# The first attention of a four-stage transformer kernel: another order of its instructions on four engines, and other PSUM banks

## What is computed

```python
h = _layernorm(x, axis=-1) * (1 + ca) + sa
x = x + ga * _L0_attn_ref(h, ...)
# inside: x = rmsnorm(h); 16 query heads, 8 key/value heads of 64
q = (x @ Wq).reshape(b, n, QH, DH).transpose(0, 2, 1, 3)
kv = x @ Wkv
q = _mh_rmsnorm(q, q_gamma)          # every head normalised to length 1, times a gamma
k = _mh_rmsnorm(k, k_gamma)
sim = jnp.tanh(sim / SOFTCLAMP) * SOFTCLAMP * DH ** (-0.5)
sim = jnp.where(causal, neg, sim); attn = jax.nn.softmax(sim, axis=-1)
out = jnp.einsum('bhgij,bhjd->bhid', attn, v) ... @ Wout   # the two query heads of a group are summed
```

## Time and profile before

| | before |
|---|---|
| median of 3 runs | 2081.79 us (2081.04 to 2085.08) |
| the profiled execution's own time | 2080.65 us |
| its span, first to last instruction | 2078.8 us |
| PE busy | 1942.7 us, 93% |
| DVE busy | 1730.8 us, 83% |
| ACT busy | 1435.2 us, 69% |
| POOL busy | 738.6 us, 36% |

### The profile page before, as it was taken

How to read it: one execution, slowest core, us unless ns; L and a number is a source line. 1 busy time by engine, 2 the same in 40 slices (tenths; PEclk the granted TensorE clock), 3 DMA queues, 4 the chain that set the end, 5 groups by cost and what they waited for, 6 DMA issues and landing times. The chain is left out here.

```text
span 2078.8 us, 41395 instructions
## 1 busy us (share of the span) xinstructions
PE 1942.7 (93%) x14878; PEld 1337.0 (64%) x14878; DVE 1730.8 (83%) x3897; ACT 1435.2 (69%) x2052; POOL 738.6 (36%) x956
## 2 busy tenths in 40 slices
PE   7899999899999999999899999999999996999998
PEld 5777777777777777777744444477777773444443
DVE  7898998998999989888476777588888886888886
ACT  3786777777777778677467777666666664666665
POOL 1554554555555555456200000045555551000000
PEclk8999999999999999999999999999999998999999
DMA  2401101101101110100076555300000000000000
GB/s 93 116 21 26 27 14 27 26 14 26 27 15 25 26 27 14 26 24 20 3 160 144 124 123 123 83 2 2 2 2 2 2 2 1 11 16 11 16 16 16
DMA packets 57001, 75.67 MB, mean 36 GB/s; under 512 B 9456, under 2 KB 34144, under 8 KB 56672
## 3 DMA queue, kind: packets, MB, share of 16 engines
q1 hardware_dynamic: 56800, 73.03, 14.8%
HBM read 51.47 MB, written 4.77 MB: 27 GB/s over the span
## 5 line engine op out<-in xcount | busy, mean ns | idle before, releaser
L504 PE MATMUL a_pS<-qs,k 128*128 128x256 f16 x1536 | 400.2, 277 | 8.5 <-issue 4.3
L524 PEld LDWEIGHTS a_pO<-va,pr 128*128 128x128 f32 x2048 | 329.2, 195 | 62.2 <-issue 48.7
L1058 POOL TENSOR_SCALAR_AFFINE_SELECT pr<-pr 128x512 f32<-128x512 f32 x256 | 227.5, 912 | 327.6 <-ACT pr L990 327.6
L524 PE MATMUL a_pO<-va,pr 128*128 128x66 f32 x2048 | 339.0, 254 | 1.3 <-POOL pr L1058 1.3
L982 ACT ACTIVATE th<-a_pS 128x1536 f32<-128x1536 f32 x128 | 185.5, 1449 | 115.9 <-PE a_pS L504 115.7
L1941 ACT ACTIVATE c_pr<-c_pS 128x1536 f32<-128x1536 f32 x128 | 185.8, 1451 | 105.7 <-PE c_pS L1739 105.7
L1985 POOL TENSOR_SCALAR_AFFINE_SELECT c_pr<-c_pr 128x512 f32<-128x512 f32 x256 | 175.7, 714 | 129.2 <-DVE c_pr L1829 129.2
L504 PEld LDWEIGHTS a_pS<-qs,k 128*128 128x128 f16 x1536 | 206.9, 136 | 22.6 <-issue 20.1
L526 PEld LDWEIGHTS a_pO<-va,pr 128*128 128x128 f32 x1024 | 162.0, 191 | 43.3 <-issue 42.5
L990 ACT ACTIVATE pr<-th 128x1536 f32<-128x1536 f32 x128 | 189.3, 1479 | 0.2
L526 PE MATMUL a_pO<-va,pr 128*128 128x66 f32 x1024 | 173.9, 251 | 0.0
(11 more groups left out here) (264 smaller groups left out, 4507.1 us busy)
## 6 DMA issues: line engine op xcount, KB each, us to landing
b_cwB<-b_by_expert SPq DMA_DIRECT2D x64, 512.0 KB, 8.5
k<-k SPq DMA_DIRECT2D x64, 256.0 KB, 3.7
x<-in_L_attn_tokens_dram SPq DMA_DIRECT2D x8, 512.0 KB, 7.0
out_dram<-x SPq DMA_DIRECT2D x16, 256.0 KB, 2.3
mb<-a_by_sample SPq DMA_DIRECT2D x31, 128.0 KB, 3.5
d_h<-in_L_ffn_h_w_dram SPq DMA_DIRECT2D x2, 1024.0 KB, 8.0
c_gb<-c_by_sample SPq DMA_DIRECT2D x1, 2048.0 KB, 7.1
b_by_expert<-b_cwT SPq DMA_DIRECT2D x64, 8.0 KB, 1.4
```

The source lines that it names most:

```text
L504: last = pe.matmul(out, (k1, k2)[part][k][:, h // G2, keys * P:(keys + 1) * P], q, start=part == 0, stop=part == 1)
L524: last = pe.matmul(out, w[:, hh * N + t * P:hh * N + (t + 1) * P], v[:, 0, p, :], start=True, stop=t == 0)
L1058: last = gp.affine_select(out=part, in_=part, compare_op=ALU.is_ge, fill=0.0, base=0, pattern=[[0, HPG], [1, P]], channel_multiplier=-1)
```

## The change

Nothing is computed otherwise, and no instruction of the first attention is added or taken away. Both loops still run from -3 to B + 1. What differs:

- the order of the steps in the loops of PE, DVE, ACT and POOL;
- the banks: `QK_BANK`, `QT_BANK`, `KT_BANK` and the others, and with them the second wait of nearly every step that writes `pW`;
- DVE adds the output of sample n - 1 to x (`dve_add`) in iteration n, before that of n - 2;
- what was one call is now cut into steps with a place of their own: the two halves of `dve_normalise`, the nine of `dve_factors` (before four and five), the two selects of a mask and the two of `gp_modulate` (the instructions were already apart);
- on ACT the take of the first values, the two upper key parts and `act_take_heads` have changed places, and tanh of group 3 follows exp of group 2 directly; the two takes of keys still stand together ahead of exp of group 2;
- `lower` for the queries (lower-q) stands twice in a row on POOL, where a `gp_sum` stood between.

The banks, the waits of the turns of keys, PE around those turns, and the whole loops of DVE and POOL:

```diff
-        QK_BANK = (1, 2, 0, 0, 1, 2)
-        QT_BANK = (2, 1, 2, 2)
-        KT_BANK, V_BANK, HB_BANK = (1, 2), (1, 2), (2, 0)
-        X_BANK, O_BANK, BACK_BANK = 1, 0, 0
+        QK_BANK = (1, 0, 1, 1, 0, 2)
+        QT_BANK = (1, 0, 0, 2)
+        KT_BANK, V_BANK, HB_BANK = (1, 0), (1, 1), (2, 2)
+        X_BANK, O_BANK, BACK_BANK = 1, 2, 2
...
             pe.wait_ge(s_lo, 2 * n + t + 1)
             if t == 0:
-                pe.wait_ge(s_va, 2 * n + 1)
+                if n + 1 < B:
+                    pe.wait_ge(s_qg, 6 * n + 9)
+                else:
+                    pe.wait_ge(s_va, 2 * n + 2)
             else:
-                pe.wait_ge(s_qs, 4 * n + 1)
+                if n + 1 < B:
+                    pe.wait_ge(s_qg, 6 * n + 8)
+                else:
+                    pe.wait_ge(s_qs, 4 * n - 1)
             out = pW[KT_BANK[t]][:, :].bitcast(F16)
             for p in range(KH):
                 last = pe.transpose(out[:, p * P:(p + 1) * P], kp[:, t, p, :], c.id16[:, :])
...
                 if n == -1:
                     keep_busy(pe, c, pS, 14)
                 pe_turn_k(pe, n + 1, 0)
-                pe_weigh(pe, n, 0, 11)
+                pe_score(pe, n, 3, 2)
+                pe_weigh(pe, n, 1, 6)
+                pe_score(pe, n, 3, 3)
+                if n == -1:
+                    keep_busy(pe, c, pS, 10)
+                pe_turn_k(pe, n + 1, 1)
+                pe_score(pe, n, 3, 4)
+                pe_weigh(pe, n, 1, 7)
+                pe_score(pe, n, 3, 5)
+                pe_score(pe, n, 3, 6)
+                pe_weigh(pe, n, 1, 8)
+                pe_score(pe, n, 3, 7)
+                pe_weigh(pe, n, 1, 9)
                 if n == -1:
                     keep_busy(pe, c, pS, 8)
                 pe_turn_q(pe, n + 1, 0)
-                pe_weigh(pe, n, 1, 0)
-                for m in range(0, 5):
-                    pe_score(pe, n, 3, m)
-                    pe_weigh(pe, n, 1, m + 1)
-                if n == -1:
-                    keep_busy(pe, c, pS, 10)
-                pe_turn_k(pe, n + 1, 1)
-                pe_score(pe, n, 3, 5)
-                pe_weigh(pe, n, 1, 6)
-                pe_score(pe, n, 3, 6)
-                pe_project_qk(pe, n + 2, 3)
-                pe_weigh(pe, n, 1, 7)
-                pe_score(pe, n, 3, 7)
+                pe_score(pe, n, 3, 8)
+                pe_out_back(pe, n - 1, 0)
+                pe_score(pe, n, 3, 9)
+                pe_score(pe, n, 3, 10)
+                pe_out_back(pe, n - 1, 1)
                 if n == -1:
                     keep_busy(pe, c, pS, 8)
                 pe_turn_q(pe, n + 1, 1)
-                pe_score(pe, n, 3, 8)
-                pe_weigh(pe, n, 1, 8)
-                pe_score(pe, n, 3, 9)
-                pe_weigh(pe, n, 1, 9)
-                pe_turn_q(pe, n + 1, 2)
-                pe_score(pe, n, 3, 10)
+                pe_score(pe, n, 3, 11)
                 pe_weigh(pe, n, 1, 10)
-                pe_score(pe, n, 3, 11)
+                pe_project_qk(pe, n + 2, 3)
                 pe_weigh(pe, n, 1, 11)
                 pe_project_qk(pe, n + 2, 4)
-                pe_weigh(pe, n, 2, 0)
                 pe_project_qk(pe, n + 2, 5)
                 if n < -1:
                     keep_busy(pe, c, pS, (5, 2)[n + 3])
...
-                dve_take_q(dve, n, 1)
-                dve_take_q(dve, n, 2)
-                dve_ln(dve, n + 2, 0)
-                dve_gain(dve, n + 1, 3)
+                dve_outputs(dve, n - 1, 2)
+                dve_mean_square(dve, n + 1)
                 dve_ln(dve, n + 2, 1)
                 dve_outputs(dve, n - 1, 3)
+                dve_gain(dve, n + 1, 3)
                 dve_gain(dve, n + 1, 4)
+                dve_sums(dve, n + 1, 1)
+                dve_outputs(dve, n - 1, 4)
+                dve_outputs(dve, n - 1, 5)
                 dve_gain(dve, n + 1, 5)
-                dve_sums(dve, n + 1, 1)
-                dve_mean_square(dve, n + 1)
+                dve_factors(dve, n + 1, 0)
+                dve_factors(dve, n + 1, 1)
+                dve_ln(dve, n + 2, 2)
+                dve_factors(dve, n + 1, 2)
+                dve_factors(dve, n + 1, 3)
+                dve_ln(dve, n + 2, 3)
+                dve_factors(dve, n + 1, 4)
+                dve_factors(dve, n + 1, 5)
+                dve_gain(dve, n + 2, 0)
+                dve_factors(dve, n + 1, 6)
+                dve_take_q(dve, n, 2)
+                dve_outputs(dve, n - 1, 6)
+                dve_factors(dve, n + 1, 7)
                 dve_take_q(dve, n, 3)
-                dve_outputs(dve, n - 1, 4)
-                dve_add(dve, n - 2)
-                dve_factors(dve, n + 1, 0)
-                dve_outputs(dve, n - 1, 5)
-                dve_gain(dve, n + 2, 0)
-                dve_gain(dve, n + 2, 1)
-                dve_ln(dve, n + 2, 2)
-                dve_outputs(dve, n - 1, 6)
-                dve_factors(dve, n + 1, 1)
                 dve_outputs(dve, n - 1, 7)
-                dve_gain(dve, n + 2, 2)
-                dve_norm(dve, n + 1, 0)
-                dve_norm(dve, n + 1, 1)
-                dve_outputs(dve, n, 0)
-                lower(dve, n + 1, 0, 0, s_lo)
-                dve_normalise(dve, n + 3)
-                dve_measure(dve, n - 2, 1)
-                lower(dve, n + 1, 0, 1, s_lo)
-                dve_outputs(dve, n, 1)
+                dve_factors(dve, n + 1, 8)
                 dve_measure(dve, n - 2, 2)
                 if n == B:
                     dve.wait_ge(s_st, ADD_STEPS * (B - 1))
                     ln_scales(dve, c, s_ls, 0, slice(0, TILES - TT))
+                dve_norm(dve, n + 1, 0)
+                dve_normalise(dve, n + 3, 0)
+                dve_outputs(dve, n, 0)
+                dve_normalise(dve, n + 3, 1)
+                lower(dve, n + 1, 0, 0, s_lo)
+                dve_norm(dve, n + 1, 1)
+                dve_outputs(dve, n, 1)
+                dve_gain(dve, n + 2, 1)
+                dve_gain(dve, n + 2, 2)
+                lower(dve, n + 1, 0, 1, s_lo)
+                dve_sums(dve, n + 2, 0)
+                dve_ln(dve, n + 3, 0)
                 dve_take_q(dve, n + 1, 0)
-                dve_sums(dve, n + 2, 0)
-                dve_outputs(dve, n, 2)
-                dve_ln(dve, n + 2, 3)
+                dve_add(dve, n - 1)
+                dve_take_q(dve, n + 1, 1)
+                dve_measure(dve, n - 1, 1)
...
-                gp_sum(gp, n - 2, 6)
-                gp_sum(gp, n - 2, 7)
-                gp_mask(gp, n - 1, 1)
-                lower(gp, n, 1, 0, s_ql)
-                gp_sum(gp, n - 1, 0)
-                lower(gp, n, 1, 1, s_ql)
-                gp_sum(gp, n - 1, 1)
-                gp_mask(gp, n - 1, 2)
-                gp_modulate(gp, n + 2)
+                gp_modulate(gp, n + 2, 1)
                 gp_sum(gp, n - 1, 2)
-                gp_mask(gp, n - 1, 3)
                 gp_sum(gp, n - 1, 3)
+                gp_mask(gp, n - 1, 3, 0)
+                gp_mask(gp, n - 1, 3, 1)
                 gp_sum(gp, n - 1, 4)
-                gp_mask(gp, n, 0)
                 gp_sum(gp, n - 1, 5)
+                gp_mask(gp, n, 0, 0)
+                gp_mask(gp, n, 0, 1)
+                gp_sum(gp, n - 1, 6)
+                gp_sum(gp, n - 1, 7)
+                gp_mask(gp, n, 1, 0)
+                gp_mask(gp, n, 1, 1)
+                lower(gp, n + 1, 1, 0, s_ql)
+                lower(gp, n + 1, 1, 1, s_ql)
+                gp_modulate(gp, n + 3, 0)
+                gp_sum(gp, n, 0)
+                gp_sum(gp, n, 1)
+                gp_mask(gp, n, 2, 0)
+                gp_mask(gp, n, 2, 1)
```

More of the change, by code:

```diff
@@ new lines, in dve_factors @@
+                last = dve.tensor_scalar(r.bitcast(I32), s.bitcast(I32), -0.5, RSQRT_MAGIC, ALU.mult, ALU.add)
+            elif step == 1:
+                last = dve.tensor_tensor(a, r, r, ALU.mult)
+            elif step == 2:
+                last = dve.tensor_tensor(a, a, s, ALU.mult)
+            elif step == 3:
+                last = dve.scalar_tensor_tensor(b, a, -10.0 / 3.0, a, ALU.add, ALU.mult)
+            elif step == 4:
+                last = dve.scalar_tensor_tensor(r, b, 5.0, r, ALU.add, ALU.mult)
+            elif step == 5:
+                last = dve.tensor_tensor(a, r, s, ALU.mult)
+            elif step == 6:
+                last = dve.scalar_tensor_tensor(b, a, -0.375 * 0.0703125, r, ALU.mult, ALU.mult)
+            elif step == 7:
+                last = dve.scalar_tensor_tensor(r, b, 0.5625, r, ALU.add, ALU.mult)
+            else:
@@ L1048, in _, with gp_mask @@
                 act_exp(act, n, 3)
+                act_square_h(act, n + 3, 0)
                 act_turned(act, n + 3)
-                act_tanh(act, n + 1, 0)
-        def gp_mask(gp, n, g):
+        def gp_mask(gp, n, g, part):
             if not 0 <= n < B:
                 return
-            gp.wait_ge(s_pr, 4 * n + g + 1)
             p = pr[g % 2]
```

(11 more changed lines are left out.)

278 lines of the change are left out of this document (138 added, 140 removed).

## The result

| | before | changed |
|---|---|---|
| median of 4 runs, us | 2083.03 (2081.04 to 2085.08) | 1969.1 (1968.53 to 1972.83) |
| profiled execution, us | 2080.65 | 1968.78 |
| its span, us | 2078.8 | 1966.9 |

The ratio is 0.9457, 95% interval 0.944 to 0.9473. The kernel is faster by 113.9 us; the forecast was about 102.

A forecast was written before the change was run, and what follows sets the result against it. PE was taken as the bound, slowed by two waits per sample and a reduced clock. Waits 76 us plus clock 30, less 4, made 101.8 us less, hence 1980 us, range 1966 to 1998.

The forecast's parts named there:

- the 27 distances: Times between successive L378 key-copy issues, third to thirtieth, one per sample: each from 30.67 to 26.90 us, 101.8 less together.
- the placement: One period of the new order laid out by PE's cadences, in us from TK0 at 0 to the next first S at 7.04.
- the waits: PE's two stalls per sample, 0.75 at the first key turn and 2.07 at TK1, both to go: 76 us.
- the clock: PE's granted clock, 0.96 before, to be full once no wait near 2 us is left: 30 us.
- The 1.10 of clock: Clock loss per sample on PE, taken as 30.67 less 29.57 us, to vanish with the long wait.
- Lower-k 1 is reached at -1.2 and goes when lower-q 0 ends, to -0.3: DVE's second lower-k waits for POOL's first lower-q, yet ends 1.1 us ahead of TK1; times relative to TK0.
- rival 1: Both lower-q on POOL hold the port in succession, lower-k 1 makes TK1 1.05 us late: 2008 us, chance 0.22.
- The five distances at the stage's ends, the fill, the drain: Parts outside the 27 distances, given no gain; another order there may take or give 3 us.
- the floor of 26.75: PE's own work per sample without the two waits, 29.57 less 2.82 us; 0.15 was added for copies and misfits.
- The swinging clock (2): PE's clock still falls with many short waits, each sample losing the 1.10 us: 2010 us, chance 0.12.
- A wait back in full (3): One PE wait returns, such as 2.07 us at QK3: 2035 to 2065 us; with both, 2081; chance 0.13.
- The slower kernel (4): Three port holds, of a norm and both lower-k, bind PE to DVE: 31.8 us a period, 2111 us, chance 0.04.

The follow-up runs named there:

- experiment 2: Kernel before with POOL's lower-q cut from 1024 to 512 elements, the lower part of the last eight query heads left zero: 1975.29 us, ratio 0.9485.
- Experiment 7: Changed kernel with ACT writing the upper queries ahead of the upper keys in both halves: 2021.0 us, ratio 0.9715.
- experiment 6: Changed kernel with the second lower-k on DVE moved behind the sums of squares: 2010.57 us, ratio 0.9654.
- Experiment 8: Changed kernel with PE's scores moved: later 1972.46 us, sooner 1979.92; last, copy wait at the second S and two W pairs parted, 1965.62.
- experiment 3: Changed kernel with one added wait at TK1: for the second lower-q, 1998.15 us; for the second gp_sum, 2082.29 us.

## Why the prediction was right, and where it was not

**The mechanism and the sum.** The period was forecast at 26.90 and is 26.99; the 27 distances at 101.8 us less, and gave 99.4. The clock in the window is 1.00. In the placement, with TK0 at 521.83, TK1 stands at +0.83 (0.84 forecast), TQ0 +2.23 (2.24), TQ1 +3.23 (3.24), QK3 +3.95 (3.97), QK4 +5.04 (5.05), the first S +7.02 (7.04). The take of queries ends 0.38 ahead of QK3 (0.5). The mask's selects stand beside the first norm and are held, as forecast.

**Waits and clock.** The terms were 76 for the waits, 30 for the clock, less 4. The rows give 66.6 of idle time and 32.8 of busy time, but the forecast counted a stall from the W's 0.17, not from its modelled end. Counted its way, with the rows of experiment 2, the waits are 74.2 (66.6 and the exposed ends, 27 x 0.28), the clock 28.7, less 3.5 for the busy time that the new order adds (726.55 less 27 x 26.78). So each term came within 2 us. The 1.10 of clock was read from two neighbouring samples, the better of them at 0.97; the sample at 1.00 takes 29.54, nearly the same.

**A step that did not come out: "Lower-k 1 is reached at -1.2 and goes when lower-q 0 ends, to -0.3".** It was reached at 520.60, which is -1.2, but it ran at once, in 0.68. The second norm came some 0.8 us sooner than I had placed it, lower-q 0 ended at 519.91 and not at 520.9, and lower-q 1 was not ready before 521.14. So the port was free, and the sign that was named for the new profile, lower-k 1 ending 0.55 behind lower-q 0, is not there. For TK1 the difference is 0.3 of spare time; for rival 1 it is its whole ground. The rival needed two lower-q one right behind the other, with lower-k behind them. Experiment 7 makes the collision with the second lower-q, and experiment 6 shows that its price was right.

**The mis-sized term: the ends.** "The five distances at the stage's ends, the fill, the drain" were given nothing, up to 3 us either way. They gave 12.5 (4.4 + 3.8 + 3.5 + 0.8); 32 copies have 31 distances, so outside the window there are four and not five. This is more than the whole miss in the total; without it the forecast would have been 2.4 us too fast. The mechanism works in those samples too, at 1.8 a distance, half of the middle's 3.7. The 4.4 ahead of the first copy are partly scatter: the repeated run of the same kernel has that copy at 42.8 and not at 44.6, while before has a single trace. The low end of the range did allow for part of it.

**The 0.09 of the period.** The usual distance is 26.87, and three of 27 are 27.6 to 27.9. In those the S stands for a late key copy, here in the timeline of PE (the repeated run has only one such, of 27.99, and so 26.94 in the mean; the tenth distance is such a long one in every trace of the changed order):

```profile
555.51 0.33 PE L533 MATMUL a_pO<-va,pr 128*128 128x66 f32 x2
556.56 0.27 PE L513 MATMUL a_pS<-qs,k 128*128 128x256 f16 x1 [0.71 <-issue]
```

The 0.12 above the floor of 26.75 that was read from the earlier trace rows is W behind W, and the first S standing 0.21 behind its W instead of 0.17, since the copy took 3.86 from issue to reader (524.99 to 528.85), as the 3.87 of the earlier trace rows. At these prices the two make 0.19, more than the 0.12, so they are the likely cause and the floor was a little lower than read. Experiment 8 took 0.13 away with two pairs and the later wait.

**The rivals.** The swinging clock (2) did not come, nor with waits of 0.6 and 1.1 put back; only with 2.1. The Trainium skill, "TensorE: Matmul & The Clock Gate", section "A second HAM failure mode: psum-queue depth-cycling", tells of a kernel whose short pauses between groups made the clock swing. No run here shows it: the changed order cycles its PSUM banks and holds 1.00. A wait back in full (3) did not come, but experiment 3 shows that its upper price was too kind: one wait of 2.1 alone gives 2082 and not 2035 to 2065, because its clock costs 1.5 a sample and not 1.10. The slower kernel (4) had no ground, for one lower-q of the two now meets nothing but the end of a norm. DVE's work is 23.1 a sample, 0.9 under the 24.0 forecast; 3.8 of the fall is the two lower-k; most of the rest is the steps of the factors (0.7) and the norms (0.2).

The rule for the port fits as well. The Trainium skill, "GPSIMD Engine Reference", section "Specifications", names DVE instructions with two SBUF inputs as those that contend with POOL. The trace agrees: gain and output, with one input from PSUM, ran at their usual 681 and 424 ns on average, also the 31 of each between 60 and 900 us that started beside a lower-q. The forecast said that the trace of before agrees for gain, but that trace could not show it: between 60 and 900 us no gain starts beside a lower-q there, only beside other steps of POOL.
